# A sixth block sum on VectorE in exchange for 128 columns of TensorE's denominator matmuls, in an fp32 attention and FFN kernel

## The chip, the cores and the metric

One core of one Trainium2 chip runs the whole program. The metric is the time of one execution on the device, in microseconds (us). Each kernel is run several times, and the median stands for it.

## The reference, cut to what matters

```
x = x + layernorm(attention(layernorm(x)))          # x: 4 batches x 512 positions x 1024, fp32
x = x + layernorm(ffn(layernorm(x)))                # 8 experts, top 2, LoRA rank 16, and a dense base

# attention: 32 query heads, 8 key/value heads of 32, rotary embedding, causal
scores = q @ k.T / sqrt(32), masked above the diagonal
attn   = softmax(scores)                            # exp(s - row max) / sum over keys
out    = attn @ v
```

The change concerns the sum over keys in the softmax, its denominator.

## The kernel before, in words

**Stages.** The kernel has three: the QKV projection (0 to about 297 us of the span), attention (about 297 to 600 us), and the output projection with the FFN, tile by tile (the rest). The change lies in attention.

**Groups.** Attention works through NG = 32 groups. A group is one batch and one key/value head with its REP = 4 query heads. Positions come in four blocks of P = 128. `SCORES` lists the ten causal pairs (key block, query block) in the order (0,0) (0,1) (0,2) (0,3) (1,1) (1,2) (1,3) (2,2) (2,3) (3,3). The exponentials of a group lie in `prob[n % 2]`, one block of 128 keys by 4 heads by 128 queries for each pair.

**Units of a step.** Step n of TensorE follows the string `ORDER` (L62), and one letter and number is one unit:

- S0 to S9: the scores of group n, key by query, one matmul of 512 columns into one of three banks (`scores`, L1370). ScalarE makes the exponentials from them (`exps`, L828).
- R0 to R10: the scores of group n + 2 again, query by key (`row_scores`, L1347), of which VectorE only takes the row maxima (`maxima`, L1007, whose instructions stand at L1018). R0 is four heads of 128 columns, R1 and R2 are two heads of 256 each, R3 to R6 one head of 384, R7 to R10 one head of 512.
- T: a transpose of the maxima of group n + 1 (L1367), which ScalarE and VectorE split into two rows (VectorE: `shift_lo`, L1026). SyncE loads them into `q_t` (`load_shift`, L484, issued at L490), and S0 of the next step waits for that.
- V0 to V3: the product with the values for group n - 1 (`weigh`, L1397).
- D: the denominators of group n - 1 (`denominators`, L1403).

```
ORDER = ("S0 R0 R1 S1 S2 V0 V1 V2 V3 R2 T R3 R4 "
         "S3 S4 S5 R5 D S6 R6 R7 S7 R8 S8 S9 R9 R10").split()
ROW_BANKS = (0, 1, 2, 7)
```

**The ring of banks.** The R units and T share four PSUM banks in turn (`ring_units`, L74). The units of a step, in their order R0 R1 R2 T R3 R4 and so on to R10, take the banks 0, 1, 2, 7, 0, 1, ... A unit may start once the unit four places before it in the ring has been read (`ring_free`, L1337). So R0 of a step waits for the maxima of R7 of the step before, R1 for those of R8, R2 for those of R9, R3 for R0, R4 for R1, R5 for R2, and R6 for T. VectorE counts a unit of maxima as done when the small instruction that reads its accumulator (DVE_READ_ACCUMULATOR2_ANT, same line) has ended.

**VectorE's step.** The loop at L1206 runs the maxima of R0, R1, R2, then `shift_lo`, R3 to R8, then `sum_last`, then R9 and R10. `sum_last` (L1203) adds the blocks (0,3) and (1,3) into `key_sum[:, 1]`.

**GpSimd's step.** The loop at L720 masks the two diagonal blocks (0,0) and (1,1) (`mask`, L697), adds (0,2) and (1,2) into `key_sum[:, 0]` (`add_keys`, L711, for which it waits on the exponentials), masks (2,2) and (3,3), and adds three more blocks to `key_sum`. The first of these three waits for `sum_last`. For steps 1 to 24 it ends with a piece of the low half of the output weights (L717).

**Denominators.** D multiplies by a matrix of ones with 32 columns, for four heads into four 32-partition parts of one bank. The sum over 128 keys is TensorE's; sums over key blocks are partly made ahead by VectorE and GpSimd (`key_sum`). Query blocks 2 and 3 come from `key_sum` (L1424, 256 columns a head). Query blocks 0 and 1 come from the blocks (0,0) and (0,1) (L1421, 256 columns a head) and then (1,1) on top (L1427, 128 columns a head). The fp32 matmul is two instructions in the trace, so a line with 4 heads shows x8.

Of the kernel before, what the change touches and what calls it, by code (L numbers as in the profile page):

```python
# [7 lines left out]
ALU = mybir.AluOpType  # L8
# [3 lines left out]
P = 128  # L12
# [4 lines left out]
TT = SEQ // P  # L17
HEADS, KV, HD = 32, 8, 32
REP = HEADS // KV
NG = BATCH * KV  # L20
# [7 lines left out]
HALF = 512  # L28
# [23 lines left out]
SCORES = [(kc, qb) for kc in range(TT) for qb in range(kc, TT)]  # L52
NS = len(SCORES)
SUMS = 4
FIRST = [SCORES.index((kc, kc)) for kc in range(TT)]
# [50 lines left out]
def wait(eng, sem, value):  # L106

    if value > 0:
        eng.wait_ge(sem, value)
# [15 lines left out]
def build(nc, x, w_qkv, b_qk, b_v, w_out, b_o, w_ffn, b_ffn, cos_t, sin_t, ident_h, row_mask_h, before_h, out):  # L125
# [7 lines left out]
    with ExitStack() as ctx:  # L133
# [3 lines left out]
        start = arena_at + 128  # L137
        limit = arena_at + arena_bytes

        def sem(name):  # L140
            return ctx.enter_context(nc.semaphore(name))
# [16 lines left out]
        m = Map(start)  # L158
        ident = m("ident", [P, P])
        ones = m("ones", [P, HD])  # L160
# [22 lines left out]
        m = Map(b_at, b_size)  # L183
# [5 lines left out]
        for j, at in enumerate((c_at, d_at)):  # L189
            m = Map(at, cd_size)  # L190
            xt_h.append(m(f"xt_h{j}", [P, KC, SEQ], F32R))
            xt_l.append(m(f"xt_l{j}", [P, KC, SEQ], F32R))
        m = Map(d_at, cd_size)
        x_first = [m(f"x_first{j}", [P, D]) for j in range(TT)]
        m = Map(e_at, e_size)
        x_ring = [m(f"x_ring{j}", [P, D]) for j in range(XRING)]
        m = Map(f_at)
# [10 lines left out]
        m = Map(b_at, b_size)  # L208
# [11 lines left out]
        m = Map(c_at, cd_size)  # L220
        for s in range(SLOTS):
            if s == SLOTS - 1:
                row_mask = m("row_mask", [P, SEQ])
                m = Map(e_at + SPILL, e_size - SPILL)
            q_t.append(m(f"q_t{s}", [P, REP, SEQ], F32R))
            k_t.append(m(f"k_t{s}", [P, SEQ], F32R))
        m = Map(d_at, cd_size + SPILL)
        prob = [m("prob0", [P, NS, REP, P])]
        m = Map(m.at + SPILL, cd_size + SPILL)
        y = m("y", [P, D])  # L230
        x1_at = m.at
        att = [m("att0", [P, SEQ])]
        m = Map(x1_at + D * 4, D * 4)
        att.append(m("att1", [P, SEQ]))
        den_sb = m("den_sb", [P, SEQ])
        m = Map(f_at, f_size)
# [4 lines left out]
        m = Map(c_at, cd_size)  # L241
# [4 lines left out]
        m = Map(m.at + 4 * FW * 4, c_at + cd_size - m.at - 4 * FW * 4)  # L246
# [8 lines left out]
        m = Map(x1_at, 2 * D * 4)  # L255
        x1 = [m(f"x1_{j}", [P, D]) for j in range(2)] + [x1_last]
        m = Map(sums_at, 2 * D * 4)
        xt2_h = m("xt2_h", [P, KC, P], F32R)
        xt2_l = m("xt2_l", [P, KC, P], F32R)
        m = Map(v_at, 2 * D * 4)  # L260
        at_raw = m("at_raw", [P, KC, P])
        den_i = m("den_i", [P, KC, P])
        m = Map(e_at + SPILL + 2 * FW * 4, e_size - SPILL - 2 * FW * 4)
# [56 lines left out]
        prob_masked = sem("prob_masked")  # L320
        prob_summed = sem("prob_summed")
        last_summed = sem("last_summed")
        den_ps = sem("den_ps")
        den_ready = sem("den_ready")
        den_stored = sem("den_stored")
# [75 lines left out]
        def den_bank(n):  # L401

            return bank[7] if n >= NG - 2 else bank[6]
# [545 lines left out]
        def _(dve):  # L949
# [73 lines left out]
            def shift_lo(n):  # L1023

                dve.wait_ge(shift_hi, n + 1)
                nc.vector.scalar_tensor_tensor(out=shift_l[n % 2][:], in0=shift_bank(n)[0:REP * TT, 0:P], scalar=-1.0,  # L1026
                                               in1=shift_h[n % 2][:].bitcast(F32), op0=ALU.mult, op1=ALU.subtract
                                               ).then_inc(shift_sb, 1)
# [61 lines left out]
            def split_att(t):  # L1090
                dve.wait_ge(at_hi, t + 1)
                nc.vector.tensor_tensor(at_l[:], at_raw[:], at_h[:].bitcast(F32), ALU.subtract).then_inc(at_ready, 1)
# [105 lines left out]
            def sum_last(n):  # L1198
# [4 lines left out]
                nc.vector.tensor_tensor(key_sum[n % 2][:, 1, :, :], p[:, SCORES.index((0, 3)), :, :],  # L1203
                                        p[:, SCORES.index((1, 3)), :, :], ALU.add).then_inc(last_summed, 1)

            for n in range(NG):  # L1206
                after = n + 2 < NG

                def maxima_of(*units):
                    if after:  # L1210
                        for i in units:
                            maxima(n + 2, i)

                maxima_of(0, 1, 2)
                if n + 1 < NG:
                    shift_lo(n + 1)
                if n == NG - 2:
                    split_att(0)
                maxima_of(3, 4, 5)
                if n >= KV and n % KV == 4:  # L1220
                    invert_sums(n // KV - 1)
                maxima_of(6, 7, 8)
                if n < NG - 1:
                    sum_last(n)
                maxima_of(9, 10)
                if n == NG - 3:
                    scale_att(0)
                if n == NG - 2:
                    dve.wait_ge(late_loaded, 16 * N_LATE)
                    split_ffn(0)  # L1230
                    project_bias(0, 0)
                if n == NG - 1:
                    split_ffn(1)
                    scale_att(1)
                    sum_last(n)
                    project_bias(0, 1)
                    y_statistics(0)
# [44 lines left out]
        def _(pe):  # L1282
            mm = nc.tensor.matmul
# [119 lines left out]
            def denominators(n):  # L1403

                pe.wait_ge(prob_masked, TT * n + TT)
                pe.wait_ge(prob_summed, SUMS * n + (SUMS if n < NG - 1 else 1))
                if n == NG - 1:
                    pe.wait_ge(last_summed, NG)
                if n < NG - 2:
                    pe.wait_ge(att_ready, n + 1)  # L1410
                elif n == NG - 2:
                    pe.wait_ge(row_max, NR * NG)
                    pe.wait_ge(shift_sb, NG)
                else:
                    pe.wait_ge(den_ready, n)
                if n == 0:
                    pe.wait_ge(const_ready, 1)
                p, total = prob[n % 2], key_sum[n % 2]
                for h in range(REP):
                    dst = den_bank(n)[HD * h:HD * h + HD, :].rearrange("p (b q) -> p b q", q=P)  # L1420
                    mm(dst[:, 0:2, :], ones[:], p[:, 0:2, h, :], start=True, stop=False, skip_group_check=True)  # L1421
                for h in range(REP):
                    dst = den_bank(n)[HD * h:HD * h + HD, :].rearrange("p (b q) -> p b q", q=P)
                    mm(dst[:, 2:4, :], ones[:], total[:, :, h, :], start=False, stop=False, skip_group_check=True)  # L1424
                for h in range(REP):
                    dst = den_bank(n)[HD * h:HD * h + HD, :].rearrange("p (b q) -> p b q", q=P)
                    last = mm(dst[:, 1:2, :], ones[:], p[:, FIRST[1]:FIRST[1] + 1, h, :], start=False, stop=True,  # L1427
                              skip_group_check=True)
                if n == NG - 1:
                    for h in range(REP):  # L1430
                        dst = den_bank(n)[HD * h:HD * h + HD, :].rearrange("p (b q) -> p b q", q=P)
                        mm(dst[:, 2:4, :], ones[:], p[:, FIRST[2]:FIRST[2] + 2, h, :], start=False, stop=False,
                           skip_group_check=True)
                    for h in range(REP):
                        dst = den_bank(n)[HD * h:HD * h + HD, :].rearrange("p (b q) -> p b q", q=P)
                        last = mm(dst[:, 3:4, :], ones[:], p[:, FIRST[3]:FIRST[3] + 1, h, :], start=False, stop=True,
                                  skip_group_check=True)
                last.then_inc(den_ps, 1)
# [32 lines left out]
            for c in range(HALVES, KC):  # L1471
                pe.wait_ge(wq_ready, c + 1)
                for p in range(2):
                    for i in range(2):
                        last = project_chunk(0, p, i, c)
# [184 lines left out]
```

## Time and profile before

| | before |
|---|---|
| time, median of 3 runs | 1018.43 us (1017.51 to 1020.02) |
| the profiled execution | 1016.17 us |
| its span, first to last instruction | 1014.4 us |
| granted TensorE clock, mean | 0.997 |
| TensorE busy | 990.1 us, 98% of the span |
| VectorE busy | 660.6 us, 65% |
| GpSimd busy | 455.2 us, 45% |
| ScalarE busy | 400.2 us, 39% |

The profiled execution took 1.8 us more than its span, for what lies around the first and last instruction. Its time is 2.3 us below the median of the three runs. "Busy" is time with at least one instruction under way, so several matmuls at once on parts of the array count once. Starts of instructions overlap the ends of those before them on the same engine: on VectorE a 128x512 maximum is listed with 0.73 us, and the next instruction starts 0.65 us after it.

### The profile page before, as it was taken

What the parts mean: (1) busy time and instruction counts of PE and PEld (TensorE: products, weight loads), DVE (VectorE), ACT (ScalarE), POOL (GpSimd) and SP (SyncE); (2) the same over time, 40 slices, a digit from 0 to 9 for tenths busy, and PEclk for the clock granted to TensorE, in tenths of its full rate; (3) what the DMA queues carried; (4) which work ended last, traced back from release to release, by engine and by line L of the source; (5) the groups of instructions that cost most, each with busy time, mean ns of one, the idle gap of its engine ahead of it and who ended that gap; (6) DMA issues with size and microseconds to landing.
All of it is one profiled execution on the core that took longest, in us unless ns stands there. A gap on an engine that the chain in (4) does not pass through costs nothing.

```text
span 1014.4 us, 17409 instructions
## 1 busy us (share of the span) xinstructions
PE 990.1 (98%) x6400; PEld 814.0 (80%) x6400; DVE 660.6 (65%) x1954; ACT 400.2 (39%) x682; POOL 455.2 (45%) x490
## 2 busy tenths in 40 slices
PE   6999999999999999999999999999999999999996
PEld 5888888898886666666666678999999999999996
DVE  7752443434558988998989666666666666666655
ACT  7331221210127777777777662222222222222211
POOL 1453542433439999999998911111111111111110
PEclk9999999999999999999999999999999999999998
DMA  9342442237247876765555463222222222222101
GB/s 354 151 146 84 146 145 84 83 116 195 99 148 197 217 197 173 186 163 151 140 140 145 138 209 99 86 83 84 83 83 84 84 84 83 83 79 77 54 22 41
DMA packets 78644, 127.23 MB, mean 125 GB/s; under 512 B 7776, under 2 KB 46944, under 8 KB 75488
## 3 DMA queue, kind: packets, MB, share of 16 engines
q1 hardware_dynamic: 78560, 126.13, 41.0%
q8 instruction: 51, 0.84, 0.3%
q14 instruction: 33, 0.27, 0.1%
HBM read 85.20 MB, written 40.37 MB: 124 GB/s over the span
## 4 chain that ended last, share of the span: by engine, by line
PE 92%; DVE 3%; DMA 2%; ACT 1%; POOL 1%; issue 1%; SPq 0%; POOLq 0%; DVEq 0%; ACTq 0%
PE bank L1287 21%; PE bank L1289 21%; PE bank L1288 21%; PE bank L1359 8%; PE bank L1381 7%; PE bank L1397 7%; DMA q_t<-shift_l 2%; PE bank L1421 2%; PE bank L1296 1%; PE bank L1547 1%; PE bank L1424 1%; PE bank L1427 1%; DVE wf_l L1195 1%; DVE bank L1018 1%; PE bank L1460 0%
## 5 line engine op out<-in xcount | busy, mean ns | idle before, releaser
L1018 DVE CUSTOM_DVE_ANT_0 bank<-bank,row_mask 128x384 f32<-128x384 f32 (+3 forms) x512 | 235.7, 517 | 49.9 <-PE bank L1359 49.8
L653 POOL TENSOR_TENSOR ln_rs<-ln_ve,minus_half 128x1 f32<-128x1 f32 x64 | 61.6, 962 | 392.6 <-DVE ln_mm L962 392.6
L837 ACT ACTIVATE prob<-bank 128x512 f32<-128x512 f32 x320 | 173.9, 599 | 34.8 <-PE bank L1381 34.5
L1287 PE MATMUL bank<-wf_h,xt_h 128*128 128x384 f32 (+1 forms) x384 | 129.7, 338 | 0.9 <-DVE z L1176 0.9
L1289 PE MATMUL bank<-wf_l,xt_h 128*128 128x384 f32 (+1 forms) x384 | 130.2, 339 | 0.0
L1288 PE MATMUL bank<-wf_h,xt_l 128*128 128x384 f32 (+1 forms) x384 | 129.6, 338 | 0.0
L1359 PE MATMUL bank<-k_t,q_t 96*128 96x384 f32 (+3 forms) x512 | 123.4, 337 | 0.4 <-DVE row_top L1018 0.3
L1287 PE MATMUL bank<-xt_h,wq_h 128*128 128x512 f32 x304 | 119.8, 394 | 0.0
L1289 PE MATMUL bank<-xt_l,wq_h 128*128 128x512 f32 x304 | 118.6, 390 | 0.0
L1288 PE MATMUL bank<-xt_h,wq_l 128*128 128x512 f32 x304 | 118.5, 390 | 0.0
L711 POOL TENSOR_TENSOR key_sum<-key_sum,prob 128x512 f32<-128x512 f32 x93 | 117.8, 1293 | 0.0
L1381 PE MATMUL bank<-q_t,k_t 98*128 98x512 f32 x320 | 110.9, 410 | 1.5 <-DMA q_t<-shift_l 1.2
L697 POOL TENSOR_SCALAR_AFFINE_SELECT prob<-prob 128x512 f32<-128x512 f32 x128 | 89.5, 708 | 31.6 <-ACT prob L837 31.2
L1287 PE MATMUL bank<-wo_h,at_h 128*128 128x512 f32 x256 | 101.2, 395 | 0.0
L1289 PE MATMUL bank<-wo_l,at_h 128*128 128x512 f32 x256 | 100.1, 391 | 0.0
L1288 PE MATMUL bank<-wo_h,at_l 128*128 128x512 f32 x256 | 100.0, 391 | 0.0
L1359 PEld LDWEIGHTS bank<-k_t,q_t 96*128 96x128 f32 x512 | 82.7, 190 | 21.5 <-DVE row_top L1018 8.7
L780 ACT CAST turn_h<-turn 128x512 fp32r<-128x512 f32 x40 | 24.9, 622 | 161.3 <-POOL turn L667 149.7
L667 POOL TENSOR_TENSOR turn<-turn 128x512 f32<-128x512 f32 x20 | 25.9, 1295 | 123.7 <-DVE turn L995 123.7
L914 ACT ACTIVATE z<-z,ln_nm,ln_rs 128x1024 f32<-128x1024 f32 (+1 forms) x17 | 20.2, 1192 | 153.0 <-POOL ln_nm L655 153.0
L1397 PE MATMUL bank<-prob,v_sb 128*32 128x512 f32 (+3 forms) x1024 | 75.5, 435 | 0.0
L1287 PEld LDWEIGHTS bank<-wf_h,xt_h 128*128 128x128 f32 x384 | 72.1, 188 | 1.8 <-DVE z L1176 1.2
(118 smaller groups left out, 1882.4 us busy)
## 6 DMA issues: line engine op xcount, KB each, us to landing
q_t<-q_scratch SPq DMA_DIRECT2D x32, 512.0 KB, 5.5
q_scratch<-turn_h SPq DMA_DIRECT2D x16, 512.0 KB, 2.7
q_scratch<-turn SPq DMA_DIRECT2D x16, 512.0 KB, 3.0
q_t<-q_scratch SPq DMA_DIRECT2D x32, 256.0 KB, 5.8
att_scratch<-att SPq DMA_DIRECT2D x32, 256.0 KB, 2.5
at_raw<-att_scratch SPq DMA_DIRECT2D x16, 512.0 KB, 3.7
x<-x SPq DMA_DIRECT2D x16, 512.0 KB, 4.2
out<-z SPq DMA_DIRECT2D x15, 512.0 KB, 2.9
```

The lines of the kernel that those rows point to most:

```text
L653: nc.gpsimd.tensor_tensor(ln_rs[j][:], ln_ve[j][:], minus_half[:], ALU.pow).then_inc(count, 1)
L667: nc.gpsimd.tensor_tensor(r[:, 0, 0, :], r[:, 0, 0, :], r[:, 0, 1, :], ALU.subtract).then_inc(rope_sum, 1)
L697: nc.gpsimd.affine_select(out=block_of, in_=block_of, compare_op=ALU.is_ge, fill=0.0, base=0, pattern=[[0, REP], [1, P]], channel_multipli ...
L711: nc.gpsimd.tensor_tensor(total, first, prob[n % 2][:, b, :, :], ALU.add).then_inc(prob_summed, 1)
L837: nc.scalar.activation(prob[n % 2][:, i, :, :].rearrange("p h q -> p (h q)"), score_bank(n, i)[:], ACT.Exp, scale=INV_SQRT_HD).then_inc(pr ...
L1018: last = nc.vector.tensor_tensor_reduce(out=row, in0=row, in1=row_mask[:, SEQ - w:SEQ], scale=1.0, scalar=LOWEST, op0=ALU.add, op1=ALU.max ...
L1287: mm(dst, a_h, w_h, start=start, stop=False, skip_group_check=True)
L1288: mm(dst, a_l, w_h, start=False, stop=False, skip_group_check=True)
L1289: return mm(dst, a_h, w_l, start=False, stop=stop, skip_group_check=True)
L1359: last = mm(dst[:, w * at:w * at + w], q_t[s][0:KROWS, h, P * qb:P * qb + P], k_t[s][0:KROWS, 0:w], start=(at == 0), stop=True, skip_group ...
L1381: mm(score_bank(n, i)[:].rearrange("p (h q) -> p h q", q=P), k_t[s][0:KROWS + 2, P * kc:P * kc + P], q_t[s][0:KROWS + 2, :, P * qb:P * qb ...
L1397: last = mm(bank[6][HD * h:HD * h + HD, P * kc:SEQ].rearrange("p (b q) -> p b q", q=P), v_sb[b % 2][:, kc, HD * g:HD * g + HD], prob[n % 2 ...
```

## The change

A sixth sum, `sum_first`, is made by VectorE for groups 0 to 29: it adds block (0,1) and the masked block (1,1) into a buffer `first_sum`, which lies where `y` of the last stage lies. It stands between the maxima of R7 and those of R8. It waits for the second mask of the group and for the denominators of group n - 2 (which last read that buffer). In D, the line L1421 then covers block (0,0) alone (128 columns a head where there were 256), and the line L1427 reads `first_sum` in place of (1,1), with the columns it had. D gets one more wait. The last two groups stay as they were.

```diff
@@ SBUF map
+        first_sum = [Map(m.at + HALF * 4 * j)(f"first_sum{j}", [P, REP, P]) for j in range(2)]
         y = m("y", [P, D])
@@ VectorE
+            def sum_first(n):
+                wait(dve, den_ps, n - 1)
+                dve.wait_ge(prob_masked, TT * n + 2)
+                p = prob[n % 2]
+                nc.vector.tensor_tensor(first_sum[n % 2][:], p[:, SCORES.index((0, 1)), :, :], p[:, FIRST[1], :, :],
+                                        ALU.add).then_inc(first_summed, 1)
...
-                maxima_of(6, 7, 8)
+                maxima_of(6, 7)
+                if n < NG - 2:
+                    sum_first(n)
+                maxima_of(8)
                 if n < NG - 1:
                     sum_last(n)
@@ TensorE, denominators(n)
+                whole = 2 if n >= NG - 2 else 1
+                if n < NG - 2:
+                    pe.wait_ge(first_summed, n + 1)
                 for h in range(REP):
-                    mm(dst[:, 0:2, :], ones[:], p[:, 0:2, h, :], start=True, stop=False, skip_group_check=True)
+                    mm(dst[:, 0:whole, :], ones[:], p[:, 0:whole, h, :], start=True, stop=False,
+                       skip_group_check=True)
...
-                    last = mm(dst[:, 1:2, :], ones[:], p[:, FIRST[1]:FIRST[1] + 1, h, :], start=False, stop=True,
-                              skip_group_check=True)
+                    second = p[:, FIRST[1]:FIRST[1] + 1, h, :] if n >= NG - 2 else first_sum[n % 2][:, h:h + 1, :]
+                    last = mm(dst[:, 1:2, :], ones[:], second, start=False, stop=True, skip_group_check=True)
```

## Rows read from the trace of the kernel before

**Rows 1.** The page, busy time of each engine over the span.
```profile
PE 990.1 (98%) x6400; PEld 814.0 (80%) x6400; DVE 660.6 (65%) x1954; ACT 400.2 (39%) x682; POOL 455.2 (45%) x490
```

**Rows 2.** Busy time by stretch: window, length, then PE, PEld, DVE, ACT, POOL, clock.
```profile
487.00:551.00 64.00, 64.00 (x592) 41.10 (x595) 57.73 (x241) 48.67 (x98) 59.60 (x63) 1.00 0.58 145
```

**Rows 3.** The chain that ended last, two steps: start, us, what.
```profile
491.69 0.57 PE bank L1421 x8
492.26 0.43 PE bank L1424 x8
492.69 0.22 PE bank L1427 x8
...
500.67 0.57 PE bank L1421 x8
```

**Rows 4.** Timeline of VectorE, maxima of R6, R8, then L1203, R1's end, R2's.
```profile
493.56 0.57 DVE L1018 CUSTOM_DVE_ANT_0 bank<-bank,row_mask 128x384 f32<-128x384 f32 x1 [0.67 <-PE bank L1359]
...
494.69 0.73 DVE L1018 CUSTOM_DVE_ANT_0 bank<-bank,row_mask 128x512 f32<-128x512 f32 x1
495.34 0.14 DVE L1018 DVE_READ_ACCUMULATOR2_ANT row_top<- 128x1 f32 x1
495.34 0.69 DVE L1203 TENSOR_TENSOR key_sum<-prob 128x512 f32<-128x512 f32 x1
495.95 0.69 DVE L1018 CUSTOM_DVE_ANT_0 bank<-bank,row_mask 128x512 f32<-128x512 f32 x1
...
498.96 0.14 DVE L1018 DVE_READ_ACCUMULATOR2_ANT row_top<- 128x1 f32 x1
499.30 0.43 DVE L1018 CUSTOM_DVE_ANT_0 bank<-bank,row_mask 128x256 f32<-128x256 f32 x1 [0.20 <-PE bank L1359]
...
500.04 0.14 DVE L1018 DVE_READ_ACCUMULATOR2_ANT row_top<- 128x1 f32 x1
```

**Rows 5.** Timeline of TensorE's weight loads: R1's two, and R5's one.
```profile
495.56 0.30 PEld L1359 LDWEIGHTS bank<-k_t,q_t 96*128 96x128 f32 x2
...
500.23 0.19 PEld L1359 LDWEIGHTS bank<-k_t,q_t 96*128 96x128 f32 x1 [0.24 <-DVE row_top L1018]
```

**Rows 6.** All instructions of L1203: duration in ns, least, median, most.
```profile
L1203 DVE TENSOR_TENSOR key_sum<-prob x32: 675/685/1352, 303.5 to 590.2; 128x512 f32<-128x512 f32 x32
```

**Rows 7.** Timeline of GpSimd: an add, the masks of (2,2) and (3,3).
```profile
493.30 1.30 POOL L711 TENSOR_TENSOR key_sum<-prob 128x512 f32<-128x512 f32 x1
494.70 0.64 POOL L697 TENSOR_SCALAR_AFFINE_SELECT prob<-prob 128x512 f32<-128x512 f32 x1
495.67 0.86 POOL L697 TENSOR_SCALAR_AFFINE_SELECT prob<-prob 128x512 f32<-128x512 f32 x1 [0.34 <-ACT prob L837]
```

**Rows 8.** Timelines of GpSimd and VectorE, step 30: an add and L1203.
```profile
575.24 1.30 POOL L711 TENSOR_TENSOR key_sum<-prob 128x512 f32<-128x512 f32 x1
...
575.74 1.35 DVE L1203 TENSOR_TENSOR key_sum<-prob 128x512 f32<-128x512 f32 x1 [0.97 <-ACT prob L837]
```

**Rows 9.** The chain again: denominators of groups 0 and 28.
```profile
309.51 0.57 PE bank L1421 x8
...
563.59 0.57 PE bank L1421 x8
```

**Rows 10.** The chain in step 0 and in a long step, where a load is on it.
```profile
300.85 2.84 DMA q_t<-shift_l
...
345.78 3.39 DMA q_t<-shift_l
```

**Rows 11.** Timeline of PE: first denominator matmuls at both ends of two long steps.
```profile
345.47 0.42 PE L1421 MATMUL bank<-prob,ones 128*32 128x256 f32 x4
...
354.93 0.42 PE L1421 MATMUL bank<-prob,ones 128*32 128x256 f32 x4
...
373.08 0.42 PE L1421 MATMUL bank<-prob,ones 128*32 128x256 f32 x4
...
382.81 0.42 PE L1421 MATMUL bank<-prob,ones 128*32 128x256 f32 x4
```

More of the change, by code:

```diff
@@ L322, in build @@
         last_summed = sem("last_summed")
+        first_summed = sem("first_summed")
         den_ps = sem("den_ps")
```

## The prediction

> **What bounds the kernel now.** The page first: TensorE is busy 98% of the span, VectorE 65% [rows 1]. That is an average over three stages, so the next view is the busy time by stretch, inside attention. From 487 to 551 us TensorE is busy all 64.00 us, VectorE 57.73 and GpSimd 59.60 [rows 2]. Three engines are near full there, and the one that bounds is TensorE, but with little to spare. The chain of waits confirms it: a step from one block of denominators to the next is 8.98 us (491.69 to 500.67) and is made of TensorE's work alone [rows 3]. The timelines then show where the engines hold each other. VectorE waits twice in a step for TensorE, 0.67 us before the maxima of R6 and 0.20 us before those of R2 [rows 4]. TensorE's weight load of R5 waits for VectorE: it starts at 500.23, right behind the end of R2's maxima at 500.04 + 0.14 = 500.18 [rows 4, 5]. So a release takes 0.05 us. And R1's first load starts at 495.56, where R8's maxima, for which it must wait, ended at 495.34 + 0.14 = 495.48 [rows 4, 5]. That spare of 0.08 - 0.05 = 0.03 us is what the change meets.
>
> **What TensorE saves.** The line L1424 has 256 columns a head and takes 0.43 us, L1427 has 128 and takes 0.22 [rows 3]. L1421 goes from the one size to the other, so 0.21 us goes for each of 30 groups, 6.3 us in all if nothing else moved. Bounds: nothing (if its first pass is held by its weight loads) and 0.21. I take 0.21, as L1427 shows that this width runs at half the time. The added wait lies ahead of D in TensorE's queue, on a semaphore that was set some 6 us earlier. I cost it at nothing; its upper bound is the 0.05 us of a release.
>
> **What VectorE adds.** `sum_first` is the same operation and shape as L1203, which takes 0.69 us and lets the next instruction start after 0.60 (495.34 to 495.95) [rows 4]. VectorE's waits of 0.67 and 0.20 could hold 0.60, if a step's sum were all that counted. But the place counts: the sum stands behind the wait at R6 and ahead of R8's maxima, and R1 waits for these.
>
> Now follow the step in the times of before, with all that follows D 0.21 earlier. R6's maxima start at 493.35 (the wait before them shrinks from 0.67 to 0.46, so TensorE still releases them). The sum starts where R8's did, at 494.69 - 0.21 = 494.48. R8's start at 495.08 and are done at 495.48 - 0.21 + 0.60 = 495.87. R1's first load can start at 495.87 + 0.05 = 495.92. Without the sum it would have started at 495.56 - 0.21 = 495.35. TensorE stands for 0.57 us, more than twice what D saved, and all behind R1 in its queue (S1, S2, the product with the values, T, R2 to R5, the next D) comes 0.36 us later than before. By this alone a step is 8.98 + 0.36 = 9.34 us.
>
> **What GpSimd adds to it.** The two engines hold each other where VectorE adds two blocks in SBUF. Mask (3,3) takes 0.86 us against 0.64 for mask (2,2), because it started at 495.67 while L1203 (from 495.34) was running. It was held until 496.53 - 0.64 = 495.89, or 0.55 us behind L1203's start [rows 4, 7]. The other way round, L1203 took 1.35 us against a median of 0.685 when it started at 575.74 inside an add. It was held until 577.09 - 0.69 = 576.40, 0.14 us before the add ended [rows 6, 8]. The Trainium skill ("SBUF — State Buffer", Who interferes with whom) calls this an exclusive lock between a VectorE instruction with two SBUF inputs and a GpSimd one that reads SBUF, the first to issue keeping the port and the other blocked. The trace agrees in both directions.
>
> In the changed step, the sum runs from 494.48. Mask (2,2) can't start before 494.70 - 0.21 = 494.49, so it comes second and is held until 494.48 + 0.55 = 495.03. It ends at 495.67. Mask (3,3) follows at about 495.64, just ahead of L1203 (495.34 + 0.39 = 495.73), and reads until 495.64 + 0.64 - 0.14 = 496.14. L1203 stands for 0.4 us. R9, R10, R0 and R1 on VectorE come 0.39 + 0.4 = 0.8 us later than before, so it is free at 498.96 + 0.8 = 499.76 at latest (I take 499.73, with 0.38 for the stand). TensorE's R2 would have its data at 499.30 + 0.36 = 499.66. So R2's maxima start at 499.73, 0.43 later than before, R5 is released 0.43 later, and the step is 8.98 + 0.43 = 9.41 us. Were L1203 first instead, it would be 9.34. I take 9.41, since mask (3,3) is ready first by 0.09 us. GpSimd's own work is 59.60/64 of 8.98, or 8.4 us, and with 0.4 of waiting it still fits.
>
> **The sum.** From the denominators of group 0 to those of group 28 there are 28 steps and 563.59 - 309.51 = 254.08 us [rows 9]. A few are long, because S0 waited for the load of the shift rows [rows 10]. Such a wait comes before R1 and covers its stand. Two are long enough to keep their length, 354.93 - 345.47 = 9.46 and 382.81 - 373.08 = 9.73 [rows 11]. The other 26 become 9.41 each. That is 26 x 9.41 + 9.46 + 9.73 = 263.85, or 9.8 us more. Step 0 has no V or D and TensorE waits there for the same load for 2.84 us of the chain [rows 10], behind which VectorE's extra 0.60 disappears, so I cost it at nothing. D of groups 28 and 29 saves up to 0.21 each with no R1 behind it; I take 0.3 off. The change costs 9.5 us. The profiled execution took 1016.17 us, which gives 1025.7; against the median of 1018.43, 2.3 us higher, it gives 1027.9. The last stage moves as a whole and is not touched.
>
> **Bounds.** If L1203 is first, 26 x 0.07 = 1.8 us less. If D saves nothing, 26 x 0.21 = 5.5 us more. If the added wait shows, 1.4 us more. Medians of this kernel spread 2.5 us. So this case reaches from 1024 to 1035.
>
> **Rivals.**
>
> - *The sum falls into VectorE's idle time (faster).* For it: 0.67 + 0.20 us idle a step against 0.60 added, and TensorE is the full engine. The place is R1's load, the price is the whole saving, 29 x 0.21 = 6.1 us, so 1012.3. It decides if R1 need not wait for R8, or if the stand at R1 stays below 0.21 us. Against it: the spare there is 0.03 us [rows 4, 5], and the idle time lies before R6 and R2, not between R6 and R1. Chance 0.07.
> - *The two just cancel (no change).* Needs a stand of about 0.21, that is a sum that costs VectorE a third of its row. Chance 0.04.
> - *The sum itself is caught behind GpSimd's add (slower still).* The add runs from 493.30 to 494.60 and by the 0.14 above reads until 494.46, and the sum starts at 494.48 [rows 7]. Each sum that is caught in full costs 1.352 - 0.685 = 0.67 us more, straight in front of R8: 28 x 0.67 = 18.7 us, so 1046.6. Against it: a longer step lets GpSimd get to its add earlier relative to D, which heals this. Here the skill's rule (same page and section) gives this price if the add is first and none if it isn't. Chance 0.07.
> - *The forecast:* 0.82.
>
> **How the numbers follow.** A measurement of this kernel can tell some 0.3%, 3 us. The forecast and the third rival lie above that, 0.89; cancelling is 0.04, faster 0.07. The range takes in the forecast's bounds with a little below for a partial stand, 1022.5 to 1035.
>
> **What would show it.** Right: TensorE's idle time gets a term "waited for DVE row_top" of about half a us a step at R1's load; the step is 9.3 to 9.45 us; D is 0.21 us shorter; L1203's median rises towards 1.07 us and mask (2,2) to about 1.2 us; VectorE's wait before R6 stays near 0.46 us. Wrong: a step of 8.77 us (R1 not held), or a mean of the new line well above 0.7 us (caught behind the add), or a step of 9.3 with L1203 at 0.69 (the order at the port misjudged).

## The result, and the profile after

| | before | after |
|---|---|---|
| median | 1017.97 us (1016.76 to 1020.02, 4 runs) | 1034.67 us (1034.29 to 1034.86, 4 runs) |
| the profiled execution | 1016.17 us | 1034.29 us |
| its span | 1014.4 us | 1032.6 us |

The changed kernel takes 1.0158 times as long (interval 1.0138 to 1.0179), 16.7 us more. The forecast was 9.5 us more. The sign is right, and the time lies in the range, 0.3 us below its top. In the changed kernel the lines move: L1018 is L1020, L1203 is L1205, the rows L1359 are L1372, the scores L1381 are L1394, the values L1397 are L1410, and D is L1437, L1441 and L1445. The new sum is L1213.

First the page after, busy time by engine, and the chain that ended last by engine:

```profile
PE 1000.1 (97%) x6400; PEld 816.1 (79%) x6400; DVE 686.8 (67%) x1984; ACT 396.8 (38%) x682; POOL 461.4 (45%) x490
...
PE 75%; DVE 17%; ACT 3%; issue 3%; POOL 1%; DMA 1%; SPq 0%; POOLq 0%; DVEq 0%; ACTq 0%
```

Busy shares hardly differ from [rows 1]: TensorE 97% for 98%, VectorE 67% for 65%. The chain says what the shares don't. VectorE now has 17% of it, where two steps of before were TensorE's alone [rows 3]. Here is one step of it (start, us, what):

```profile
515.68 0.47 DVE first_sum L1213
516.14 0.69 DVE bank L1020
...
516.89 0.96 DVE key_sum L1205
517.85 0.61 DVE bank L1020
...
520.98 0.44 PE bank L1372
521.42 0.70 PE bank L1394 x3
522.12 0.17 PE bank L1372
522.29 0.35 PE bank L1437 x8
...
531.85 0.36 PE bank L1437 x8
```

A step is 531.85 - 522.29 = 9.56 us, D's first line takes 0.35 us for 0.57, and from 515.7 to 520.9 VectorE is on the chain without a break: the sum, R8, L1205, R9, R10, R0, R1 (the rows of the last four are left out). Then it passes to TensorE at 520.98, which is R4. The timelines of VectorE and of GpSimd in that step (start, us, instruction, and in brackets the idle time before it):

```profile
514.40 0.57 DVE L1020 CUSTOM_DVE_ANT_0 bank<-bank,row_mask 128x384 f32<-128x384 f32 x1 [0.46 <-PE bank L1372]
...
515.54 0.69 DVE L1213 TENSOR_TENSOR first_sum<-prob 128x512 f32<-128x512 f32 x1
516.14 0.69 DVE L1020 CUSTOM_DVE_ANT_0 bank<-bank,row_mask 128x512 f32<-128x512 f32 x1
516.75 0.14 DVE L1020 DVE_READ_ACCUMULATOR2_ANT row_top<- 128x1 f32 x1
516.75 1.10 DVE L1205 TENSOR_TENSOR key_sum<-prob 128x512 f32<-128x512 f32 x1
...
520.79 0.13 DVE L1020 DVE_READ_ACCUMULATOR2_ANT row_top<- 128x1 f32 x1
```

```profile
515.61 1.70 POOL L699 TENSOR_SCALAR_AFFINE_SELECT prob<-prob 128x512 f32<-128x512 f32 x2
```

This is the forecast's picture at the port. The sum takes its bare 0.69 us. The two masks behind it take 1.70 us for twice 0.64, L1205 takes 1.10 (forecast 1.07), and VectorE's wait before R6 is 0.46, as forecast (0.55 to 0.57 in other steps). The weight loads show who is held:

```profile
516.94 0.30 PEld L1372 LDWEIGHTS bank<-k_t,q_t 96*128 96x128 f32 x2 [0.39 <-DVE row_top L1020]
...
520.98 0.19 PEld L1372 LDWEIGHTS bank<-k_t,q_t 96*128 96x128 f32 x1 [0.31 <-DVE row_top L1020]
...
522.22 0.16 PEld L1437 LDWEIGHTS bank<-prob,ones 128*32 128x32 f32 x8 [0.29 <-issue]
```

R1's load is held, as forecast: 516.94 is 0.05 behind the end of R8's maxima (516.75 + 0.14), and 4.27 us behind the first load of D (522.22 - 9.55 = 512.67). There is a second stand that the forecast does not have: R4's load at 520.98, just behind the end of R1's maxima (520.79 + 0.13 = 520.92). In the waits of 310 to 590 us this kind leads for TensorE's loads and matmuls (total us, times, longest):

```profile
PEld bank L1372 <- DVE row_top L1020: 18.3, 53, 1.1
...
PE bank L1372 <- DVE row_top L1020: 6.3, 20, 1.0
```

**Where the 18.2 us of span came from.** The chain gives the denominators of groups 0 and 28:

```profile
310.99 0.36 PE bank L1437 x8
...
579.50 0.35 PE bank L1437 x8
```

- Ahead of D of group 0: 310.99 - 309.51 = 1.5 us [rows 9]. Of this 1.2 lies ahead of attention, where nothing that runs was changed (it is TensorE's clock at the start, see below), and 0.3 in step 0.
- The 28 steps: 268.51 for 254.08, so 14.4 us (forecast 9.8). 22 of them are 9.55 us. The three in which VectorE also inverts sums are 9.43. Three are 10.0 to 10.1, in which the new sum was caught behind GpSimd's add, as in the third rival: it took 1.40, 1.50 and 1.39 us.
- From D of group 28 to D of group 30: 29.8 for 27.95, so 1.9 us (forecast 0.3 less). Half a us of it is the step with the last sum; most of the rest lies between the D of groups 29 and 30, below.
- The rest: 0.4 us.

All instructions of the two lines, least, median and most in ns, show how rare a caught sum is (median 686, most 1498) and how regular L1205's stand (median 1100):

```profile
L1213 DVE TENSOR_TENSOR first_sum<-prob x30: 673/686/1498, 304.0 to 582.3; 128x512 f32<-128x512 f32 x30
L1205 DVE TENSOR_TENSOR key_sum<-prob x32: 673/1100/1102, 305.4 to 608.0; 128x512 f32<-128x512 f32 x32
```

### The profile page after: what moved, and what is told of

Same layout as the page of the kernel before. It is cut to its first block, busy times and chain, and to the rows that moved or that the text cites. A ratio compares the mean times of both kernels' runs of the same rounds, so it can differ in the third digit from the quotient of the medians.

```text
span 1032.6 us, 17496 instructions
## 1 busy us (share of the span) xinstructions
PE 1000.1 (97%) x6400; PEld 816.1 (79%) x6400; DVE 686.8 (67%) x1984; ACT 396.8 (38%) x682; POOL 461.4 (45%) x490
## 4 chain that ended last, share of the span: by engine, by line
PE 75%; DVE 17%; ACT 3%; issue 3%; POOL 1%; DMA 1%; SPq 0%; POOLq 0%; DVEq 0%; ACTq 0%
PE bank L1300 20%; PE bank L1302 20%; PE bank L1301 20%; DVE bank L1020 8%; PE bank L1394 3%; PE bank L1372 3%; DVE key_sum L1205 2%; DVE row_top L1020 2%; PE bank L1410 2%; PE bank L1309 2%; ACT prob L839 2%; DVE first_sum L1213 1%; PE bank L1564 1%; PE bank L1441 1%; PE bank L1437 1%
## 5 line engine op out<-in xcount | busy, mean ns | idle before, releaser
L1020 DVE CUSTOM_DVE_ANT_0 bank<-bank,row_mask 128x384 f32<-128x384 f32 (+3 forms) x512 | 235.8, 515 | 38.5 <-PE bank L1372 38.4
L1372 PE MATMUL bank<-k_t,q_t 96*128 96x384 f32 (+3 forms) x512 | 133.6, 342 | 8.2 <-DVE row_top L1020 6.7
L1394 PE MATMUL bank<-q_t,k_t 98*128 98x512 f32 x320 | 114.6, 420 | 1.0 <-DMA q_t<-shift_l 0.9
L1372 PEld LDWEIGHTS bank<-k_t,q_t 96*128 96x128 f32 x512 | 86.5, 189 | 34.5 <-DVE row_top L1020 19.5
L699 POOL TENSOR_SCALAR_AFFINE_SELECT prob<-prob 128x512 f32<-128x512 f32 x128 | 95.2, 762 | 22.9 <-ACT prob L839 21.4
L1394 PEld LDWEIGHTS bank<-q_t,k_t 98*128 98x128 f32 x320 | 58.0, 190 | 24.0 <-ACT prob L839 8.2
L1410 PE MATMUL bank<-prob,v_sb 128*32 128x512 f32 (+3 forms) x1024 | 75.5, 435 | 0.0
```

What stands on the lines that cost most here:

```text
L699: nc.gpsimd.affine_select(out=block_of, in_=block_of, compare_op=ALU.is_ge, fill=0.0, base=0, pattern=[[0, REP], [1, P]], channel_multipli ...
L1020: last = nc.vector.tensor_tensor_reduce(out=row, in0=row, in1=row_mask[:, SEQ - w:SEQ], scale=1.0, scalar=LOWEST, op0=ALU.add, op1=ALU.max ...
L1372: last = mm(dst[:, w * at:w * at + w], q_t[s][0:KROWS, h, P * qb:P * qb + P], k_t[s][0:KROWS, 0:w], start=(at == 0), stop=True, skip_group ...
L1394: mm(score_bank(n, i)[:].rearrange("p (h q) -> p h q", q=P), k_t[s][0:KROWS + 2, P * kc:P * kc + P], q_t[s][0:KROWS + 2, :, P * qb:P * qb ...
L1410: last = mm(bank[6][HD * h:HD * h + HD, P * kc:SEQ].rearrange("p (b q) -> p b q", q=P), v_sb[b % 2][:, kc, HD * g:HD * g + HD], prob[n % 2 ...
```

## The experiments

### Each half alone

**d_only**: D as in the changed kernel, but no sum; the block (0,1) is left out of the denominators of query block 1.

```diff
@@ TensorE, denominators(n), from the kernel before
+                whole = 2 if n >= NG - 2 else 1
-                    mm(dst[:, 0:2, :], ones[:], p[:, 0:2, h, :], start=True, stop=False, skip_group_check=True)
+                    mm(dst[:, 0:whole, :], ones[:], p[:, 0:whole, h, :], start=True, stop=False,
+                       skip_group_check=True)
```

> The change without the sixth sum: D multiplies block (0,0) alone and then block (1,1) unsummed, so block (0,1) is left out of the denominators of query block 1; VectorE's and GpSimd's work is that of before. This prices the saving by itself. Theory (the saving is 0.21 us a step and comes through, since everything behind D moves with it): the step goes from 8.98 to 8.77 us, 30 x 0.21 = 6.3 us less, about 1011.7. Rival (VectorE or GpSimd is already so near that TensorE's saving is not cashed in): a step above 8.9 and 1015 or more, with new waits of TensorE for row_top or key_sum.

Measured: 1014.85 us (10 runs) beside 1017.70 (13), ratio 0.9977 (0.9965 to 0.9989). So 2 to 3 us come through, of the 6 expected. The undisturbed step is 8.82 us for 8.98 (8.75 where GpSimd has no piece of the output weights), so D's saving is real. But the 28 steps take 253.3 for 254.1. The trace is of the slowest of the ten executions, 1017.8 us, yet these steps are not what made it slow: TensorE's clock was at its lower level for 3.4 us at 15.1 us and again at 574.9, both outside them. The waits of 309 to 572 us show the rest; first d_only, then the kernel before:

```profile
PEld bank L1391 <- DMA q_t<-shift_l: 8.3, 13, 1.2
```

```profile
PEld bank L1381 <- DMA q_t<-shift_l: 4.3, 9, 0.9
```

28 steps of 8.80 would be 246.4, and 28 of 8.98 would be 251.4. So in this execution 5.0 us were saved, and the longer steps give 4.2 back (6.9 over the undisturbed sum, for 2.7 before). The wait behind them is S0's for the shift rows, 8.3 us in 13 times for 4.3 in 9: the faster TensorE reaches that load before its data.

**sum_only**: the sum is made and not used; D stays as it was (`whole = 2`, no wait).

> The sixth sum at its place between R7 and R8, but D as before (256 columns, block (1,1) as it is, no wait for the sum), so the sum is made and not used. This prices the sum by itself. Theory (a chain on VectorE from R6 over R7, the sum, R8, L1205, R9, R10, R0, R1 to TensorE's R4 sets the step; D's length adds to it): the step is 9.55 + 0.21 = 9.76 us, about 6 us above the changed kernel, 1040 to 1041. Rival (D's extra wait for the sum costs something in the changed kernel): less than that, by up to 3 us. Rival (VectorE's or GpSimd's own full time bounds the step and D's length doesn't matter): the same as the changed kernel, 1034.7.

Measured: 1039.9 us, ratio 1.0223 (1.0208 to 1.0238). The steps are 9.76 us, as expected, one with a caught sum 10.11. That is 0.21 more than with the shorter D: D's saving counts in full in a step that VectorE sets, since D lies ahead of R6, whose scores VectorE waits for. D has no wait for the sum here, and the 0.21 is D's length alone, so in the changed kernel that wait costs nothing that shows.

### Which stand sets the step

**sum_after_r8**: the sum between R8's maxima and L1205.

```diff
@@ VectorE, from the changed kernel
-                maxima_of(6, 7)
+                maxima_of(6, 7, 8)
                 if n < NG - 2:
                     sum_first(n)
-                maxima_of(8)
```

> The changed kernel with the sum behind R8's maxima, straight ahead of L1205, instead of ahead of R8's. R1 of the next step is then not held. Theory of the prediction (what sets the step is TensorE standing at R1, 0.57 us): the step falls to 9.2 us or less, and the time to 1025 or less. Theory after the trace (the stand at R1 is absorbed, and TensorE's R4, which waits for R1's maxima at the end of VectorE's chain, sets the step): the chain has the same pieces in another order, so the step stays at 9.5 to 9.7 and the time at 1033 to 1038, while R1's load comes 0.5 us earlier than in the changed kernel.

Measured: 1034.0 us, ratio 1.0165 (1.0148 to 1.0183). The steps are 9.60 to 9.61 us. R1's load is no longer held: it comes 3.86 us behind D's first, for 4.27. So the stand at R1 can go without the step getting shorter. It does not set the step. A load of the same step names what does:

```profile
529.60 0.19 PEld L1371 LDWEIGHTS bank<-k_t,q_t 96*128 96x128 f32 x1 [0.58 <-DVE row_top L1020]
```

The load at 529.60 is R4's again, 0.58 us idle, ahead of the three scores S3 to S5.

**r4_later**: the changed kernel with R4 behind S3 to S5, so that less of TensorE's work stands behind R1's maxima.

```diff
@@ ORDER, from the changed kernel
-ORDER = ("S0 R0 R1 S1 S2 V0 V1 V2 V3 R2 T R3 R4 "
-         "S3 S4 S5 R5 D S6 R6 R7 S7 R8 S8 S9 R9 R10").split()
+ORDER = ("S0 R0 R1 S1 S2 V0 V1 V2 V3 R2 T R3 "
+         "S3 S4 S5 R4 R5 D S6 R6 R7 S7 R8 S8 S9 R9 R10").split()
```

> The changed kernel with one unit moved in TensorE's order: R4 behind S3, S4 and S5 in place of ahead of them. Nothing else changes, the ring of banks keeps its order. Theory (R4's wait for R1's maxima, 0.5 us into TensorE's queue with S3 to S5 and D behind it, is what sets the step of 9.55): S3 to S5, 0.70 us, now run during that wait, and the next release in line decides, R5's by R2's maxima, which the prediction had worked out as 9.41 us; so the step is 9.35 to 9.45 and the time 1029 to 1031. Rival (VectorE is simply full, or D's added wait costs the 0.14 us): the step stays at 9.55 and the time at 1034.

Measured: 1036.46 us, ratio 1.0184 (1.0163 to 1.0205), no faster than the changed kernel. (The trace is of the fastest of its four executions, 1033.78 us, in which the clock stayed up.) But the undisturbed step is 9.43 us, where the forecast, which followed only R2's maxima, had 9.41. The time goes elsewhere. Timeline of PE, four starts of D:

```profile
319.02 0.43 PE L1437 MATMUL bank<-prob,ones 128*32 128x128 f32 x8
...
328.97 0.43 PE L1437 MATMUL bank<-prob,ones 128*32 128x128 f32 x8
...
338.40 0.42 PE L1437 MATMUL bank<-prob,ones 128*32 128x128 f32 x8
...
348.36 0.43 PE L1437 MATMUL bank<-prob,ones 128*32 128x128 f32 x8
```

Steps of 9.95, 9.43 and 9.96 us. Over most of the stage one of 9.43 is followed by one of 9.95, in which the sum takes 1.3 us, caught behind the add. A step of 9.43 is too short for GpSimd: its add then starts 1.77 us behind D, for 1.48 after a long step. The long step gives it time, and so on in turn. The cure of one hold brings back the other, worth 0.5 us every second step.

**early_t_sum**: the changed kernel with T ahead of R2 (the edit of early_t, below), which makes TensorE's part of a step 0.19 us shorter.

> The changed kernel, sum and all, with the transpose moved as in early_t. There TensorE needed 0.19 us less a step. Theory (in the changed kernel the step is set by VectorE's chain from R6 to R1's maxima, and TensorE has spare time, so TensorE's 0.19 us brings nothing before R4; only what lies between R4 and D counts, some 0.1 us): step 9.4 to 9.55, time 1030 to 1034, well above the kernel before. Rival (the sum costs its own amount wherever TensorE stands, and the move gains 4 us on any kernel of this kind): 1030 as well for the whole, but with undisturbed steps of 9.36 us.

Measured: 1035.16 us, ratio 1.0165 (1.0136 to 1.0195). The undisturbed step is 9.55 us, unchanged: TensorE's time is no longer what counts there. Two steps were 11.6 us long, with the sum caught (1.54 us) and the clock at its lower level (below); the trace is of the slowest of four executions, 1038.18 us.

### What the port costs

**mask_after_l1205**: mask (3,3) waits for L1205, so that L1205 goes first.

```diff
@@ GpSimd, mask(n, kc), from the changed kernel
+                if kc == 3 and n < NG - 1:
+                    pool.wait_ge(last_summed, n + 1)
```

> The changed kernel with one more wait on GpSimd: the mask of (3,3) waits for L1205 of the same group, so that it can't start 0.07 us ahead of it and hold it. GpSimd's next add waited for L1205 anyway. Theory (L1205's stand of 0.41 us behind that mask is on the chain that sets the step): L1205 falls from 1.10 to 0.69 us, R4's load comes about 0.35 us earlier, the step is 9.2 to 9.35 and the time 1025 to 1029. Rival (the order at the port does not matter, since GpSimd's work only moves): a step of 9.5 and 1034; or GpSimd then runs late, its add catches the sum in more steps, and the time rises above 1035.

Measured: 1050.16 us, ratio 1.0321 (1.0304 to 1.0338). L1205 is bare now, median 680 ns. The sum is not:

```profile
L1215 DVE TENSOR_TENSOR first_sum<-prob x30: 683/1578/1591, 304.3 to 598.1; 128x512 f32<-128x512 f32 x30
```

Where GpSimd ends a step with a piece of the output weights, the mask's wait makes it late for its next add: the sums of groups 2 to 25 are all caught, most at 0.9 us, and the step is 10.25 us. Behind the last such piece, the two steps with the sums of groups 26 and 27 have both sums bare and are 9.35 us, where the changed kernel has 9.55: the 9.34 that the forecast had for L1205 first. So, in these two steps, L1205's stand is worth 0.20 us, not 0.07: with it goes the hold of R4, which the forecast did not have.

**one_input**: in place of the sum an instruction of the same length with one input in SBUF (the statistics of block (1,1)); (0,1) is left out of the denominators of query block 1.

```diff
@@ VectorE, sum_first(n), from the changed kernel
-                nc.vector.tensor_tensor(first_sum[n % 2][:], p[:, SCORES.index((0, 1)), :, :], p[:, FIRST[1], :, :],
-                                        ALU.add).then_inc(first_summed, 1)
+                nc.vector.bn_stats(ln_st[0][:, n % 2, :], p[:, FIRST[1], :, :].rearrange("p h q -> p (h q)")
+                                   ).then_inc(first_summed, 1)
```

> The changed kernel with the sum replaced by an instruction of the same length on VectorE that reads one block in SBUF and not two (statistics of the block (1,1), 128x512, 0.69 us); D reads (1,1) unsummed, so block (0,1) is left out of the denominators. VectorE's chain keeps its length, but nothing at the sum's place can collide with GpSimd. Theory (the collision of two-input adds costs: mask (2,2) held by the sum, the sum held by GpSimd's add after the steps with a reciprocal): no instruction at the sum's place takes over 0.75 us, mask (2,2) is back at 0.64 us, no step is 10 us long, and L1205 is still held by mask (3,3), by about 0.3 us; step 9.45, time 1030 to 1032. Rival (only VectorE's own time counts): the same step of 9.55 and 1034. A step below 9.3 would say that L1205 too is held only because of the sum.

Measured: 1029.88 us, ratio 1.0127 (1.0112 to 1.0142). The timelines of VectorE and GpSimd:

```profile
531.27 0.69 DVE L1213 BATCH_NORM_STATS2 ln_st<-prob 128x6 f32<-128x512 f32 x1
...
532.47 1.06 DVE L1205 TENSOR_TENSOR key_sum<-prob 128x512 f32<-128x512 f32 x1
```

```profile
531.39 0.63 POOL L699 TENSOR_SCALAR_AFFINE_SELECT prob<-prob 128x512 f32<-128x512 f32 x1
532.36 0.63 POOL L699 TENSOR_SCALAR_AFFINE_SELECT prob<-prob 128x512 f32<-128x512 f32 x1 [0.34 <-ACT prob L839]
```

The mask at 531.39 begins inside the statistics and takes its bare 0.63 us. That a VectorE instruction with one SBUF input leaves GpSimd alone is also the rule of the Trainium skill ("SBUF — State Buffer", Who interferes with whom), and this row agrees. Mask (3,3) still comes 0.1 us ahead of L1205 and holds it. No sum is caught, and the steps are 9.50 to 9.54 us. By the ratios, 1.0127 for 1.0158, some four fifths of the loss are VectorE's 0.60 us in that place and the hold of L1205 that it leads to; the new sum's own contention is the rest, some 3 us, and the three caught sums are half of that.

**sum_in_gap**: the sum in VectorE's idle time, ahead of R6's maxima, with mask (1,1) made ahead of (0,0) (and the values' matmuls waiting for both), so that it is ready.

```diff
@@ GpSimd and VectorE, from the changed kernel
-                mask(n, 0)
                 mask(n, 1)
+                mask(n, 0)
...
                 maxima_of(3, 4, 5)
+                if n < NG - 2:
+                    sum_first(n)
...
                 maxima_of(6, 7)
-                if n < NG - 2:
-                    sum_first(n)
                 maxima_of(8)
```

> The changed kernel with the sum moved to where VectorE has its longest idle time, between the maxima of R5 and R6, and with GpSimd masking (1,1) ahead of (0,0), so that the sum's operand is ready there. Rival of the prediction (0.60 us fits the idle time if only it is put there): R6's maxima start on time, the step falls under 9.0 and the time to 1018 or less. Theory (the sum's operand becomes ready just when GpSimd starts the next mask, which keeps the port until it has read its block, so the idle time passes unused): the sum takes about 1.1 us, R6's maxima start 0.5 us late, the step is 9.2 to 9.6 and the time 1026 to 1036.

Measured: 1039.8 us, ratio 1.0217 (1.0199 to 1.0235), slower than the change and above what was expected. The sum takes 1.02 us there (it starts inside a mask of GpSimd's), the add behind it 1.73 for 1.29, and L1205 is held as before, 1.17 us. The steps are 9.63 to 9.65 us, and three of 10.15 where VectorE also inverts sums. The idle time before R6 is 0.46 us, and a sum that occupies VectorE for 0.9 does not fit.

### A shorter TensorE step without the sum

**early_t**: the kernel before, with T ahead of R2.

```diff
@@ from the kernel before
-ORDER = ("S0 R0 R1 S1 S2 V0 V1 V2 V3 R2 T R3 R4 "
+ORDER = ("S0 R0 R1 S1 S2 V0 V1 V2 V3 T R2 R3 R4 "
@@ ScalarE
-                if 0 < n < NG - 1:
-                    copy_values(n - 1)
                 if n + 1 < NG:
                     shift_to_hi(n + 1)
+                if 0 < n < NG - 1:
+                    copy_values(n - 1)
@@ VectorE (and shift_lo(0) behind R2 of group 1)
-                maxima_of(0, 1, 2)
+                maxima_of(0, 1)
                 if n + 1 < NG:
                     shift_lo(n + 1)
+                maxima_of(2)
```

> The kernel before (no sixth sum), with the transpose of the maxima moved: T ahead of R2 in TensorE's order, ScalarE's copy of it ahead of its copy of the values, and shift_lo ahead of R2's maxima, in VectorE's idle time there. The load of the shift rows can start some 0.6 us earlier. Theory (the steps longer than 8.98 us are those in which S0 waits for that load, 2.6 us in all): they vanish, the 28 steps fall from 254.1 to about 251.5 us, and the time by 2 to 3 us, to 1015. Rival (the load is late for traffic on the DMA queues, not for its start): no change within 1 us.

Measured: 1012.47 us (1012.37 to 1013.65) beside 1016.93 (1015.42 to 1018.69), ratio 0.9958 (0.9946 to 0.9970). It beats both kernels, but not for the reason expected. The waits for the shift rows are what they were (4.3 us in 9 times at the loads). What is shorter is the undisturbed step, 8.79 for 8.98. First the chain of the kernel before, then that of early_t:

```profile
498.83 0.43 PE bank L1359 x2
499.26 0.11 PE bank L1367
499.38 0.34 PE bank L1359 x2
499.72 0.70 PE bank L1381 x3
500.43 0.25 PE bank L1359
```

```profile
503.97 0.21 PE bank L1368
504.18 0.58 PE bank L1360 x4
504.77 0.68 PE bank L1382 x3
505.45 0.17 PE bank L1360
```

T, R2, R3 and R4 take 0.79 for 0.88, and R5 0.17 for 0.25. The second has its cause in the ring. With T ahead of R2, R5's bank is T's, and R5 no longer waits for R2's maxima [rows 5]. Why the first is 0.09 shorter is not settled; T now stands next to the values' matmuls, and no run takes that apart.

**early_t_d_only**: early_t and d_only together ((0,1) again left out).

> The same move of the transpose on top of the kernel with the shorter D and no sum (block (0,1) is left out of the denominators). There 28 steps took 253.3 us although the undisturbed ones had fallen to 8.75 to 8.82. Theory (TensorE's saving of 0.21 us a step was given back where S0 waits for the shift rows): with the load started earlier the saving comes through, the 28 steps take 246 to 248 us, and the time is 1008 to 1011. Rival (GpSimd bounds the step with 8.6 us of work in a row): steps of 8.82 and more, 1012 or above.

Measured: 1011.47 us (1009.50 to 1014.31), ratio 0.9950 (0.9934 to 0.9965). Its interval overlaps that of early_t, and 1008 to 1011 had been expected. So what D saves, even without a sum to pay for it, is about one us here, no more than the noise; the undisturbed steps are 8.71 to 8.77, and GpSimd now reaches mask (3,3) in time to hold L1205 in many of them (0.7 to 0.9 us).

## Why the prediction was right and wrong

**What held.** The sign and the first half of the mechanism: TensorE held at R1, and the two engines holding each other at the port. D's 0.21 us; the sum at its bare 0.69; R1's load held (4.27 us behind D, where the forecast's 495.92 - 491.62 is 4.30); the order at the port, with L1205 at 1.10 for 1.07; VectorE's wait before R6 at 0.46 to 0.57; next to nothing in step 0 (0.3 us). The faster rival fell with R1's hold. D's saving was whole, so that bound did not come true. That is why it is luck that the time lies in the range: the top of 1035 was made of two things that did not happen (D saves nothing, 5.5 us; the added wait shows, 1.4 us), and they just covered what did.

**The step that failed.** The prediction says "R2's maxima start at 499.73, 0.43 later than before, R5 is released 0.43 later, and the step is 8.98 + 0.43 = 9.41 us". That made the term of 26 x 9.41 in the sum too small. The prediction followed VectorE's 0.8 us only as far as R2's maxima and R5. But R1's maxima are late by the full 0.8, and they release R4, with S3 to S5 and R5 still to come ahead of D. The spare there was in the trace of before. This is the load of R3 and R4:

```profile
499.10 0.30 PEld L1359 LDWEIGHTS bank<-k_t,q_t 96*128 96x128 f32 x2
```

R4's is the second, at 499.40 - 0.19 = 499.21, and R1's maxima were done at 499.10 [rows 4]. It had 0.06 us to spare above the 0.05 of a release. With R1's maxima done at 499.90, R4's load comes at 499.95. From there to D the chain after needs 0.44 + 0.70 + 0.17 = 1.31 us. That gives 501.26, and a step of 501.26 - 491.69 = 9.57 us, for 9.55 measured. So the hold at R4 is worth 0.14 us a step over the forecast. r4_later shows it by taking it away (9.43 us with L1205 still held), sum_after_r8 by taking R1's hold away without any gain, and early_t_sum by making TensorE shorter without any gain. The stand at R1 is still there (0.54 us: it comes 4.27 behind D's first load, where the forecast had 495.35 - 491.62 = 3.73 without the sum), but swallowed: by it alone the step would be 9.34, and VectorE is later than that anyway.

**The sums by terms.** 28 steps of 9.55 instead of the forecast's mix are 267.4 - 263.85 = 3.6 us more. Two of the forecast's steps were to keep a length of 9.46 and 9.73 for the shift rows' load, but in a step of 9.55 that wait is covered as well. The three caught sums add 0.46 + 0.55 + 0.45 = 1.5, and the three shorter steps take off 0.4. Together 4.6 to 4.7 us, the miss in the 28 steps.

**The third rival** was given 0.07, all or nothing, with the reason that a longer step heals it. It comes true in part: 3 of 28 steps in the changed kernel. Two of them follow the steps with the inverted sums, in which mask (3,3) is held (1.26 us), the step is short and GpSimd falls behind. The third follows a step (group 15) in which L1205's record is normal but GpSimd's next instruction begins 0.29 us later than elsewhere. It is no accident of one execution: sum_only, sum_after_r8, one_input, r4_later and mask_after_l1205 have the same 0.29 us more at the same group. Its cause is not settled. That the other sums were free was close. One of them, timelines of GpSimd and VectorE:

```profile
533.43 1.28 POOL L713 TENSOR_TENSOR key_sum<-prob 128x512 f32<-128x512 f32 x1
```

```profile
534.64 0.69 DVE L1213 TENSOR_TENSOR first_sum<-prob 128x512 f32<-128x512 f32 x1
```

The sum starts 0.07 us ahead of the add's end (up to 0.11 elsewhere), within the 0.14 in which the add no longer reads; the three caught ones start 0.25 to 0.36 ahead of it. In the changed kernel the step behind a caught one is free again each time. So the healing is real, but it works one step later, and r4_later shows both states in turn.

**The end of attention** was taken as 0.3 us less and costs 1.9 more. Half a us is the last sum's step. The most of the rest is the clock. In step 30 TensorE stands for 2.55 us before D, waiting for GpSimd's last add, and shortly after its granted clock is at the lower level. First the timeline of PE:

```profile
589.56 0.41 PE L1437 MATMUL bank<-prob,ones 128*32 128x128 f32 x5 [2.55 <-POOL key_sum L713]
...
592.04 0.63 PE L1300 MATMUL bank<-wo_h,at_h 128*128 128x512 f32 x1
```

Then two stretches (the number behind the busy times is the granted clock):

```profile
589.50:591.00 1.50, 1.44 (x24) 1.04 (x24) 1.04 (x1) 0.00 (x0) 1.50 (x2) 0.74 0.45 175
591.00:593.60 2.60, 2.60 (x9) 2.09 (x7) 1.04 (x2) 1.67 (x3) 2.46 (x4) 0.50 0.06 17
```

A 512-column matmul takes 0.63 us there, for 0.40 just after it. In the kernel before, TensorE stood for 1.95 us in the same place, until 573.20, and the clock stayed at 1.00 behind it:

```profile
575.00:577.00 2.00, 2.00 (x10) 1.65 (x10) 1.26 (x1) 1.72 (x4) 2.00 (x3) 1.00 0.03 9
```

From D of group 29 to D of group 30 the twelve traces fall into three kinds. Where the clock stayed up it is 18.0 to 18.8 us (the kernel before, r4_later, mask_after_l1205, early_t). Where it fell for 3.4 us it is 19.6 to 19.9 (the changed kernel, d_only, sum_after_r8, one_input, sum_in_gap, early_t_d_only), and where it fell for 6.8 us, 20.8 and 21.1 (early_t_sum, sum_only). So 1.4 us of the 1.9 go with the clock, all but the half us of the step before. Whether the change brings the fall about is open: d_only and early_t_d_only have it without a sum, r4_later has the sum and not the fall.

**Ahead of attention** 1.2 us more were seen in code that is the same. It is the clock again, at the start of the program. The first matmuls of the projection, before and after:

```profile
13.45 0.71 PE L1452 MATMUL bank<-xt_h,wq_h 128*128 128x256 f32 x4 [1.25 <-ACT xt_h L765]
```

```profile
13.57 1.19 PE L1469 MATMUL bank<-xt_h,wq_h 128*128 128x256 f32 x4 [1.25 <-ACT xt_h L767]
```

In the traces of the changed kernel, mask_after_l1205 and early_t_d_only these take 1.19 us for 0.71, and in those of d_only and early_t_sum the clock fell just behind them, for 3.4 us. In these five, D of group 0 lies at 310.9 to 311.4 us, in the other seven at 309.4 to 310.4. The two groups follow no edit, so this part of the 18.2 us is not the change's.

## What to carry to other kernels

A saving on a full engine can be paid back at its next wait. d_only shows it: in its trace 5.0 us were saved on TensorE and 4.2 returned, most of it at one load, and by the medians 2 to 3 us of 6 came through. When an instruction is added on the second engine, follow the delay to every unit that waits for it, each with all the work still queued behind it, and compare the sums. The first wait that is met (R1) need not set the step, nor the last (R2 to R5): here it was the one with the longest tail, R1's maxima to R4. Two engines that share a port may change places once a third wait is moved, so a gain worked out for one order of theirs (9.43) may come only every second step. And before a difference of one or two us between two traces is explained, the clock of each is looked at: 2.6 of the 18.2 us here were the clock's.

## What had not been expected of the hardware

- The order at the port can alternate with a period of two steps: 9.43 and 9.95 us in r4_later. With one more wait it stays in the bad order for 24 steps (sum 1.58 us, step 10.25), and goes back to the good one (9.35) in the steps where GpSimd has its piece of 1.0 us less to do.
- TensorE's granted clock fell to 0.50, its 1.2 GHz level, for some 3.4 us (to 593.6 in the changed kernel; the 0.74 of the stretch ahead puts its start at 590.2) after 2.55 us without a matmul. It did not in r4_later after the same 2.55 us, nor after 2.77 in mask_after_l1205. After 1.95 or 1.96 us it stayed up in the kernel before and in early_t, and fell in d_only and early_t_d_only. In early_t_sum it fell inside attention, after a gap of 1.05 us behind a caught sum, and the step was 11.6 us long where other steps with a caught sum are 10.0 to 10.1. The length of the gap alone does not tell. The timeline of PE and the stretch in early_t_sum:

```profile
430.73 0.50 PE L1373 MATMUL bank<-k_t,q_t 96*128 96x256 f32 x2 [1.05 <-DVE row_top L1020]
```

```profile
431.00:434.50 3.50, 3.50 (x20) 1.10 (x23) 3.29 (x17) 1.08 (x2) 3.13 (x3) 0.52 1.05 281
```
